# Two stages of a graph network kernel (layer tables and layer update), each run group by group of seven node blocks instead of operation by operation over all nodes

## The reference, cut to what matters

```python
for i in range(4):
    Q = _ln(h @ Wq[i], gq[i], bq[i])
    K = _ln(h @ Wk[i], gk[i], bk[i])
    qi = Q[src]; kj = K[dst]
    score = (qi * kj).sum(-1) + 0.1 * (edge_attr * qi[:, :40]).sum(-1) + logm[dst]
    ...
    m = h[dst] @ Wm[i]
    aggi = segment_sum(alpha[:, None] * m, src)
    z = concatenate([h, aggi], -1) @ Wu[i]
    z = where(z > 0, z, 0.01 * z)
    h = _ln(h + z, go[i], bo[i])
```

## Time and profile before

| | |
|---|---|
| Median of three runs | 16044.26 us (15996.3 to 16061.89) |
| The profiled execution, its own time | 16038.97 us |
| Its span, first to last instruction | 16037.2 us |
| Mean granted TensorE clock | 0.747 |
| VectorE busy over the span | 11232.7 us, 70% |
| TensorE busy over the span | 8737.8 us, 54% |

### The profile page before, as it was taken

The page is one execution under the profiler, slowest core; times in us unless marked ns, Lnnn a source line. Parts: engine busy times, 40 slices in busy tenths (PEclk is TensorE's granted clock), DMA queues, the critical chain, the costliest instruction groups (busy, mean ns, idle before and its releaser), DMA issues. The chain is left out here.

```text
span 16037.2 us, 385944 instructions
## 1 busy us (share of the span) xinstructions
PE 8737.8 (54%) x112803; PEld 7259.8 (45%) x112803; DVE 11232.7 (70%) x27212; ACT 5167.2 (32%) x15454; POOL 8942.3 (56%) x11086
## 2 busy tenths in 40 slices
PE   2011015555543379947994799479916666543342
PEld 1011013333330268846883688378814444343332
DVE  6986027777866569966996699679945544459788
ACT  0000012222220046614662466146613343323222
POOL 6787777777757334403440344034427777637365
PEclk9855556666655599959996999699957787785665
DMA  3523346666672276617661766176612222262543
GB/s 112 191 80 103 99 104 114 115 114 115 115 88 50 36 259 175 175 31 259 175 175 45 255 175 174 54 245 174 175 33 65 66 63 63 53 204 78 135 131 58
DMA packets 1458756, 1976.62 MB, mean 123 GB/s; under 512 B 412088, under 2 KB 1125944, under 8 KB 1451645
## 3 DMA queue, kind: packets, MB, share of 16 engines
q1 hardware_dynamic: 1074802, 1326.68, 26.2%
q0 software_dynamic: 309216, 511.82, 18.9%
q10 hardware_dynamic: 74552, 135.95, 2.6%
HBM read 1245.76 MB, written 614.07 MB: 116 GB/s over the span
## 5 line engine op out<-in xcount | busy, mean ns | idle before, releaser
L684 POOL DMA_INDIRECT attend_rows<-key_rows,attend_fetch_now x1824 | 1749.2, 959 | 2058.7 <-PE attend_seg L1717 1731.8
L1761 ACT ACTIVATE attend_hot<-attend_lane_hot,attend_share 128x128 f32<-128x128 fp8e4 x7296 | 2228.5, 388 | 1229.6 <-DVE attend_share L1784 961.1
L684 POOL DMA_INDIRECT edges_rows<-raw,edges_perm_now x1824 | 1854.6, 1017 | 636.5 <-issue 625.8
L684 POOL DMA_INDIRECT keys_rows<-table,keys_staged x1564 | 1649.4, 1055 | 470.7 <-issue 470.4
L1717 PE MATMUL attend_seg<-attend_rows,attend_hot 128*128 128x49 f32 x14592 | 1818.1, 279 | 132.4 <-ACT parts_layer L1765 115.9
L1717 PEld LDWEIGHTS attend_seg<-attend_rows,attend_hot 128*128 128x128 f32 x14592 | 1735.7, 195 | 213.3 <-issue 199.3
L684 POOL DMA_INDIRECT mlp_xin<-table,mlp_staged x1564 | 1510.8, 966 | 472.7 <-issue 469.6
L1704 PE MATMUL attend_qx<-attend_table,attend_oht 128*128 128x90 bf16 x21888 | 1094.0, 207 | 72.9 <-DMA attend_oht<-src_hots 71.2
L1528 POOL COPY expand_table<-k 128x156 bf16 x912 | 289.3, 317 | 1495.9 <-issue 708.7
L1801 DVE TENSOR_REDUCE attend_mraw<-attend_top 128x2 f32<-128x1024 f32 x912 | 1110.0, 1217 | 15.4 <-PE attend_top L1737 11.0
L684 POOL DMA_INDIRECT tally_rows<-rows_by_source,tally_origin_now x912 | 882.6, 968 | 299.5 <-issue 234.0
(11 more groups left out here) (547 smaller groups left out, 22374.3 us busy)
## 6 DMA issues: line engine op xcount, KB each, us to landing
key_rows<-expand_out SPq DMA_DIRECT2D x304, 624.0 KB
attend_ea<-edge_attrs SPq DMA_DIRECT2D x912, 160.0 KB
attend_table<-q SPq DMA_DIRECT2D x1832, 67.5 KB
expand_oht<-dst_hots SPq DMA_DIRECT2D x304, 384.0 KB, 3.8
attend_oht<-src_hots SPq DMA_DIRECT2D x912, 128.0 KB
attend_lane_hot<-src_hots_by_edge SPq DMA_DIRECT2D x912, 128.0 KB
raw<-keys_rows ACTq DMA_DIRECT2D x46, 2176.0 KB
rows_by_source<-spread_out SPq DMA_DIRECT2D x152, 576.0 KB, 4.8
```

Of the source, the lines that this page charges most:

```text
L684: return nc.gpsimd.indirect_dma_start(out=out, out_offset=None, in_=table, in_offset=bass.IndirectOffsetOnAxis(ap=index, axis=0))
L1761: ins = nc.scalar.activation(hot[p][:, u, c, :], lane_hot8[r][:, u, c, :], ACT.Copy, scale=share[p][:, u, c:c + 1])
```

## The change

Both stages are rewritten without `Projector` and `Norm`. All work is cut into seven groups of seven blocks (336 elements of 48-feature data per partition), and every group goes through its own chain.

In the tables stage the fourteen units of projection (seven of h, seven of q) are interleaved by the list `UNITS`. TensorE turns unit n and then multiplies unit n-1. VectorE does for a group of h `take_h` (reads the product in PSUM, centres Q, makes both variances), then one group later `finish_h` (scales, gain, bias, `k3` rows and their split), and three groups later `take_q` (split of the `q3` rows). ScalarE takes over the copies that build the `q3` rows. It also loads Wq, gq and bq, while SyncE loads the other three, and each consumer waits for its own load only. In the update stage VectorE scales `ha` group by group, ScalarE copies h into it, and `take` and `finish` run one group apart. The copies of whole products out of PSUM are gone. Per layer the tables stage issues 181 VectorE instructions where there were 56, and the update stage 105 where there were 29.

```diff
 def layer_tables(nc, k, i, layer):
+    GN = NT // GRP
+    UNITS = [("h", 0), ("h", 1), ("h", 2), ("q", 0), ("h", 3), ("q", 1), ("h", 4), ("q", 2), ("h", 5), ("q", 3), ("h", 6), ("q", 4), ("q", 5), ("q", 6)]
...
             def _(sp):
-                sp.dma_start(wqk[:, 0:F], of("Wq").rearrange("l a b -> (l a) b")).then_inc(s_w, 16)
-                sp.dma_start(wqk[:, F:], of("Wk").rearrange("l a b -> (l a) b")).then_inc(s_w, 16)
...
+                sp.dma_start(wqk[:, F:], of("Wk").rearrange("l a b -> (l a) b")).then_inc(s_wk, 16)
...
             def _(pe):
-                pe.wait_ge(s_ready, 1)
...
-                proj_.pe(pe, lambda t: k.h[:, t, :], F, wqk[:], 2 * F)
-                pe.wait_ge(s_q, 1)
-                proj_.pe(pe, lambda t: q[:, t, :], F, wu[:], F + 1)
+                def turn(n):
+                    kind, g = UNITS[n]
+                    if kind == "q":
+                        pe.wait_ge(s_q, g + 1)
+                    if n >= 2:
+                        pe.wait_ge(s_tc, n - 1)
...
+                def product(n):
+                    kind, g = UNITS[n]
+                    pe.wait_ge(s_tc, n + 1)
+                    if n >= 2:
+                        before, g_before = UNITS[n - 2]
+                        pe.wait_ge(s_taken_h if before == "h" else s_taken_q, g_before + 1)
...
+                for n in range(2, len(UNITS)):
+                    turn(n)
+                    product(n - 1)
+                product(len(UNITS) - 1)
...
             def _(act):
...
+                def result(n):
+                    kind, g = UNITS[n]
+                    if kind == "h":
+                        act.wait_ge(s_var, g + 1)
+                        nc.scalar.activation(root[:, g], stat[:, g], ACT.Sqrt).then_inc(s_root, 1)
+                    else:
+                        act.wait_ge(s_p, n + 1)
+                        after(act, s_split, g - 1)
+                        nc.scalar.activation(half[g % 2][:, :, 0:F], psp[n % 2][:, :, 0:F], ACT.Copy)
+                        nc.scalar.activation(half[g % 2][:, :, F + 1], psp[n % 2][:, :, F], ACT.Copy).then_inc(s_taken_q, 1)
+                        nc.scalar.activation(half[g % 2][:, :, KDOT:], q[:, groups_of(g), 0:RBF], ACT.Copy, scale=0.1).then_inc(s_half, 1)
+
+                for n in range(len(UNITS)):
+                    act.wait_ge(s_t, n + 1)
+                    if n >= 2:
+                        act.wait_ge(s_p, n - 1)
+                    nc.scalar.activation(st[n % 2][:], pst[n % 2][0:F], ACT.Copy).then_inc(s_tc, 1)
+                    if n >= 2:
+                        result(n - 2)
...
             def _(dve):
+                def take_h(n, g):
+                    at = groups_of(g)
+                    dve.wait_ge(s_p, n + 1)
+                    pq, pk = psp[n % 2][:, :, 0:F], psp[n % 2][:, :, F:2 * F]
+                    ch.step(v.tensor_reduce(avg[:], pq, AX, ALU.add))
+                    ch.done(v.tensor_copy(sq[:], pk))
+                    ch.done(v.tensor_tensor(sq[:], sq[:], pk, ALU.mult))
+                    ch.step(v.tensor_reduce(stat[:, g, 0], sq[:], AX, ALU.add))
+                    ch.done(v.tensor_scalar(avg[:], avg[:], 1.0 / F, None, ALU.mult))
+                    ch.done(v.tensor_tensor(uc[:, at], pq, bc(avg[:], F), ALU.subtract))
+                    dve.sem_inc(s_taken_h, 1)
+                    ch.done(v.tensor_tensor(sq[:], uc[:, at], uc[:, at], ALU.mult))
+                    ch.done(v.tensor_reduce(stat[:, g, 1], sq[:], AX, ALU.add))
+                    ch.done(v.tensor_scalar(stat[:, g], stat[:, g], 1.0 / F, EPS, ALU.mult, ALU.add))
+                    dve.sem_inc(s_var, 1)
+
+                def finish_h(g):
+                    at = groups_of(g)
+                    dve.wait_ge(s_root, g + 1)
+                    ch.done(v.reciprocal(stat[:, g], root[:, g]))
+                    ch.step(v.tensor_tensor(uc[:, at], uc[:, at], bc(stat[:, g, 1], F), ALU.mult))
+                    ch.step(v.tensor_tensor(row[:, at, 1:1 + F], k.h[:, at], bc(stat[:, g, 0], F), ALU.mult))
+                    ch.step(v.tensor_copy(row[:, at, 0], stat[:, g, 0]))
+                    ch.done(v.tensor_copy(row[:, at, KROW - 1], root[:, g, 0]))
+                    ch.step(v.tensor_tensor(uc[:, at], uc[:, at], rows_of(gq[:], GRP), ALU.mult))
+                    k3 = [k.k3[:, j].rearrange("p (t w) -> p t w", w=KROW)[:, at] for j in range(3)]
+                    ch.done(v.tensor_copy(k3[0], row[:, at]))
+                    ch.step(v.tensor_tensor(q[:, at], uc[:, at], rows_of(bq[:], GRP), ALU.add))
+                    ch.done(v.tensor_tensor(rest_k[:], row[:, at], k3[0], ALU.subtract))
+                    dve.sem_inc(s_q, 1)
+                    ch.done(v.tensor_copy(k3[1], rest_k[:]))
+                    ch.done(v.tensor_tensor(k3[2], rest_k[:], k3[1], ALU.subtract))
+
+                def take_q(g):
+                    dve.wait_ge(s_half, g + 1)
+                    split_group(v, ch, half[g % 2][:], [k.q3[:, groups_of(g), j, :] for j in range(3)], rest_q[:])
+                    dve.sem_inc(s_split, 1)
+
+                take_h(0, 0)
+                take_h(1, 1)
+                finish_h(0)
+                take_h(2, 2)
+                finish_h(1)
+                for g in range(3, GN):
+                    take_h(2 * g - 2, g)
+                    finish_h(g - 1)
+                    take_q(g - 3)
+                finish_h(GN - 1)
+                for g in range(GN - 3, GN):
+                    take_q(g)
...
 def layer_update(nc, k, i, layer):
...
                 dve.wait_ge(s_prod, 1)
...
-                proj_.dve(dve, z, F)
-                ch.done(v.tensor_scalar(lz[:], z[:], 0.01, None, ALU.mult))
-                ch.done(v.tensor_tensor(z[:], z[:], lz[:], ALU.max))
-                ch.done(v.tensor_tensor(z[:], z[:], k.h[:], ALU.add))
-                dve.wait_ge(s_w, 80)
-                norm.dve(dve, ch, z[:], k.h[:], go[:], bo[:])
...
+                def take(g):
+                    at = groups_of(g)
+                    dve.wait_ge(s_p, g + 1)
+                    got = psp[g % 2][:, :, 0:F]
+                    ch.done(v.tensor_scalar(lz[:], got, 0.01, None, ALU.mult))
+                    ch.done(v.tensor_tensor(z[:, at], got, lz[:], ALU.max))
+                    dve.sem_inc(s_taken, 1)
+                    ch.done(v.tensor_tensor(z[:, at], z[:, at], k.h[:, at], ALU.add))
...
+                def finish(g):
+                    at = groups_of(g)
+                    dve.wait_ge(s_root, g + 1)
+                    ch.done(v.reciprocal(stat[:, at], root[:, at]))
+                    ch.done(v.tensor_tensor(z[:, at], z[:, at], bc(stat[:, at], F), ALU.mult))
+                    ch.done(v.tensor_tensor(z[:, at], z[:, at], rows_of(go[:], GRP), ALU.mult))
+                    ch.done(v.tensor_tensor(k.h[:, at], z[:, at], rows_of(bo[:], GRP), ALU.add))
+
+                take(0)
+                for g in range(1, GN):
+                    take(g)
+                    finish(g - 1)
+                finish(GN - 1)
```

More of the change, by code:

```diff
@@ new lines, in product @@
+                def product(g):
+                    pe.wait_ge(s_tc, g + 1)
+                    if g >= 2:
+                        pe.wait_ge(s_taken, g - 1)
+                    for m in range(GRP):
+                        ins = nc.tensor.matmul(psp[g % 2][:, m, 0:F], st[g % 2][:, m, :], wz[:], start=True, stop=True)
+                    ins.then_inc(s_p, 1)
+                turn(0)
+                pe.wait_ge(s_w, 16)
+                nc.tensor.transpose(psp[1][0:F, 0, 0:F], wm[:], k.ident[0:F, 0:F]).then_inc(s_wt, 1)
```

183 lines of the change are left out of this document (118 added, 65 removed).

## The result

| | before | the change |
|---|---|---|
| median | 16034.35 us (15996.3 to 16061.89, 4 runs) | 15861.98 us (15842.11 to 15882.66, 4 runs) |
| ratio | 1 | 0.9884, 95% interval 0.9862 to 0.9905 |
| the profiled execution, own time | 16039 us | 15882.66 us, span 15880.9 us |
| four tables stages | 539.9 us | 430.7 us |
| four update stages | 267.0 us | 211.9 us |

The change makes the kernel 1.2% faster: 172 us by the medians. I measure a stage from the start of its first own instruction or load to the end of VectorE's last. The eight stages took 806.9 us and now take 642.6 us. The rest of the program hardly moved, so the time came from where the edit was made. Of the 38.4 us that the first tables stage lost (142.7 to 104.3), 4.9 us are its head: the first product was taken 13.3 us after the first load before, and is taken 8.4 us after it now.

The account below looks back on a forecast made before the run. Taken as bound: TensorE and VectorE parts one behind the other in eight stages. Heads, group work and stalls give tables 105.0 and update 53.4 us, four layers 634 instead of 806.9 us, so 15866 us; range 15800 to 15935 us.

Parts of the forecast that it names:

- Bound: Tables and update stages, 806.9 us of 16037.2: no engine fills them; TensorE and VectorE parts follow one another and could overlap.
- Work of a group: VectorE's instructions for one group: 11.9 us in tables (83.2 for seven), 6.24 us in the update (43.7 for seven).
- Stalls: VectorE's waits after the head: 0.7 + 2 x 4.0 + 3 x 0.5 + 2.9 = 13.1 us in tables, 0.3 us in update.
- Heads: Time from a stage's start until VectorE takes the first product: 8.7 us in tables, 9.4 us in the update.
- This leaves 8.7 us: Tables head: 13.3 us before, less 3.0 us by waiting for Wk alone and 1.62 us for the earlier first turn.
- VectorE's first reduction 3 us earlier: Sign at the tables stage's head: the reduction waits for Wk only, not for all six loads.
- Sum: Four layers of tables 105.0 us and update 53.4 us: 634 us in place of 806.9, 173 us less, so 15866 us.
- TensorE at 2.4 GHz: Rival: higher clock in both stages, tables 95.4 us and update 50.9 us, so 15817 us; chance 0.12.
- Less hidden: Rival: the 4.0 us tables stall returns in the three groups given 0.5 us, 42 us more, so 15908 us; chance 0.16.
- Dearer short instructions: Rival: each of 804 more VectorE instructions costs 0.1 us extra, so 15946 us; chance 0.12.
- Engines in turn: Rival: s_q chains the engines, nothing overlaps; tables 150 us, update 76 us, 906 us in all, 99 more; chance 0.03.
- The rule against the change: Advice of tiles of at least 512 elements: fixed parts of 201 more instructions a layer cost 126 us, 16165 us if nothing hides.

Follow-up runs that it names:

- e1: The tables stage as changed, layer_update as in the kernel before; 15892.93 us, ratio 0.9914 to the kernel before.
- e2: The update stage as changed, layer_tables as in the kernel before; 15985.72 us, ratio 0.9975 to the kernel before.
- e3: Against the changed kernel, TensorE multiplies unit n-1 before it turns unit n where n is a q unit; 15828.15 us, ratio 0.9866.
- e5: Against the changed kernel, the loop over layers is written out as four copies of the code; 15887.9 us, ratio 0.9882.
- e8: Against the changed kernel, the update's second half is done once over all 49 blocks after the seven takes; 15898.15 us in one run.
- e9: Against the changed kernel with h's product first and q casts cut on both sides, ScalarE squares k instead of VectorE; 15836.49 us in one run.
- e10: The changed kernel with h's product first, q casts cut on both sides, update's second half whole, layers written out; 15813.36 us, ratio 0.9842.

## Why the prediction was right, and where it was off

**Bound.** It rested on TensorE's and VectorE's parts lying one behind the other. In the changed stages VectorE does 45 us more work and they are 164 us shorter, so the gain is overlap. e1 and e2 show each part of the change to give its share by itself.

**Work of a group.** 83.2 us for seven groups of the tables, 82.6 measured; 43.7 us for the update, 44.0 measured (53.7 less 9.7). The casts of `k3` took 0.34 and 0.35 us (0.35), those of q 0.81 (0.81), an operation of seven elements 0.16 to 0.17 (0.16). Prices split into a fixed part and a rate, from instructions of 336 and 2352 elements, carried over to instructions of 7, 364 and 630.

**Stalls.** 13.1 us forecast in a tables stage, 13.2 measured: 0.75 (0.7), twice 4.08 (4.0), three times 0.61 (0.5) and 2.51 (2.9). e3 shows their cause.

**Heads: the mis-sized term.** "This leaves 8.7 us" held for the first layer (8.4) and not for the others (12.9, 13.2 and 12.6). The text took VectorE to be ready when Wk lands, from rows of the first stage only the earlier trace rows, though a loop runs the stage four times. It cost 4.2 + 4.5 + 3.9 = 12.6 us. e5 shows that the loop's branch back causes it. The sign "VectorE's first reduction 3 us earlier" came in the first layer (2.4 us after the first load, 5.4 before) and not in the second (6.9, 6.3 before). The update's head came at 9.7 us in the first layer, against 9.4 and a stall of 0.3 us somewhere behind it; no such stall came.

**Sum.** The stages were to take 634 us and took 642.6: 12.6 us more in three heads, 4 x 0.6 us less in the groups' work, 1.7 us less in the updates. The forecast of 15866 us lies 4 us over the median. That is closer than the method deserves: of the 12.6 us that the heads cost more, 4.1 us were made up by terms that were forecast too long, and the rest of the program moves by more than the remainder from run to run.

**Rivals.** TensorE at 2.4 GHz (15817 us) did not come: seven of eight stages at 0.50. The rival gave 50.9 us for an update; the updates of this order took 51.4 to 52.0 us at mean clocks of 0.53 to 0.63, and none here ran at full clock throughout. Less hidden (15908 us) did not come; the three waits where it was to show are 0.61 us. Dearer short instructions (15946 us) did not come: the gaps between chained instructions stayed at 0.03 to 0.04 us, and the groups' work at the forecast sum. Engines in turn did not come either; its sum is 4 x (150 + 76) = 904 us, not 906.

**The rule against the change.** The Trainium skill, "VectorE: DVE Perf Modes", section "The TRN2 errata", advises tiles of at least 512 elements. Its price is right here (0.507 us by the prediction's estimate from that page, 0.50 to 0.51 us in the trace), and its advice alone is not enough: e8 gives back 3.8 us of busy time for 24 instructions, 0.157 us each, while the staggered tables gained 109 us in four stages with 125 instructions more in each. Cutting pays where it opens work of another engine to overlap; the updates' second half opened nothing and would have been better whole.

## What to carry to other kernels

Where two engines work one behind the other on a whole tile, cut into groups and stagger, but cut only the steps that another engine waits for. In the in-order queue of the producer, put what waits for nothing ahead of what waits for a signal of the consumer: this order alone was worth 9.4 us in 104 (e3), and the same order in ScalarE's queue took back most of what e9 saved. When a shorter wait is forecast in a loop's body, read the head of the second pass too: the cover that is taken away may have hidden the branch back. Before a sum of waits under one label is read as a finding, look for the single row that makes it (e5).

## What the runs showed of the hardware that was not expected

- After the layer loop's branch back, VectorE's first instruction came 3.4 us after SyncE's first load, the second 2.3 us later still, each after a wait with no releaser, and ScalarE's first load 5.1 us after SyncE's; with the layers written out the waits are gone and the two first loads are 0.01 us apart (e5).
- A cast of 7 x 90 elements with both sides cut in rows took 533 ns, where half of 630 elements at the full rate (0.157 us and 315 x 1.043 ns) would be 0.486 us. Four rows of 90 would give 0.532 us, and 25 of 49 rows 2.504 us, which is the 2.503 us of the earlier trace rows. That the odd row is not halved fits both sizes; it was not tried with an even count.
- The stages that VectorE bounds hardly depend on TensorE's clock: an update of e10 took 47.4 us at 0.64 and the one of 49.0 us ran at 0.50, where the old update took 56.7 and 70.8 us.
